# A four-layer gated cross-attention and feed-forward program on one core: another order of work in the first expert layer

## The reference

```
x = x + tanh(g_xattn[n]) * attention_n(layernorm(x), ctx)
x = x + tanh(g_ffn[n])   * ffn_n(layernorm(x))
```

```
scores = sigmoid(x @ gate_w.T)                 # 64 experts in 8 groups; 4 groups are kept
idx, w = top 6 of the kept experts, w scaled to sum 2.5
shared = relu(x @ su.T)**2 @ sd.T              # 512 hidden features, for every token
slot   = rank of the token among the tokens of its expert; 64 slots per expert
yd[e]  = relu(xd[e] @ w1[e].T)**2 @ w2[e].T    # xd[e]: the 64 token rows of expert e
out    = shared + sum over the 6 experts of w * yd[e, slot]
```

## Time and profile before

| | us |
|---|---|
| median of 3 runs | 2621.82 |
| range | 2613.22 to 2622.74 |
| profiled execution | 2621.67 |
| its span | 2619.9 |
| TensorE busy in the span | 2358.4 (90%) |

### The profile page before, as it was taken

One profiled execution on the slowest core, in us unless ns is written; L12 is line 12 of the kernel. 1 busy time (PEld: TensorE's weight loads), 2 busy tenths in 40 slices (PEclk: granted clock), 3 DMA queues, 4 the chain that ended last, 5 costly groups with the idle time before them and its releaser, 6 DMA issues. The chain is left out here.

```text
span 2619.9 us, 31016 instructions
## 1 busy us (share of the span) xinstructions
PE 2358.4 (90%) x11508; PEld 1603.2 (61%) x11508; DVE 1589.5 (61%) x2529; ACT 1044.5 (40%) x1517; POOL 1452.7 (55%) x850
## 2 busy tenths in 40 slices
PE   7879999899999986699799999969997999999778
PEld 6657777655555544466455555567886555555467
DVE  4654442367777756966677777632225777777442
ACT  3433333244545432411344545423332554554333
POOL 1431110057878874346387878843442687887733
PEclk9889898599999997689799999979998999999879
DMA  1034443301111103100111111022211111111010
GB/s 33 1 123 141 136 148 120 97 18 54 36 51 38 36 9 131 36 14 1 54 36 53 36 52 37 7 62 71 89 37 48 36 36 52 38 36 42 1 51 20
DMA packets 50128, 138.52 MB, mean 53 GB/s; under 512 B 7757, under 2 KB 13597, under 8 KB 49404
## 3 DMA queue, kind: packets, MB, share of 16 engines
q1 hardware_dynamic: 49596, 136.22, 16.9%
q10 hardware_dynamic: 384, 0.33, 0.1%
HBM read 123.32 MB, written 13.21 MB: 52 GB/s over the span
## 5 line engine op out<-in xcount | busy, mean ns | idle before, releaser
L2080 DVE TENSOR_REDUCE mx<-psum 128x1 f32<-128x500 f32 x1008 | 643.8, 675 | 248.0 <-PE psum L1186 245.6
L1615 ACT ACTIVATE E<-psum 125x896 f32<-125x896 f32 x576 | 527.5, 919 | 665.8 <-PE psum L1207 657.0
L1843 POOL TENSOR_TENSOR SA<-SA,E 125x896 f32<-125x896 f32 x288 | 611.3, 2123 | 22.6
L1215 PE MATMUL psum<-E,V 125*64 125x448 f32 x2304 | 472.4, 545 | 0.0
L1186 PE MATMUL psum<-K,Q 128*128 128x500 f32 x1008 | 370.1, 416 | 30.3 <-DVE mx L2080 9.4
L1205 PE MATMUL psum<-Q,K 128*125 128x448 f32 x1152 | 345.7, 381 | 8.9 <-DVE Q L2020 7.2
L1207 PE MATMUL psum<-Q,K 128*125 128x448 f32 x1152 | 329.6, 367 | 0.0
L1843 POOL TENSOR_TENSOR SA<-SA,SB 125x896 f32<-125x896 f32 x96 | 202.6, 2111 | 194.6 <-DVE SB L2100 190.5
L1215 PEld LDWEIGHTS psum<-E,V 125*64 125x64 f32 x2304 | 152.6, 136 | 231.0 <-issue 221.4
L1205 PEld LDWEIGHTS psum<-Q,K 128*125 128x125 f32 x1152 | 203.0, 187 | 136.4 <-issue 107.2
L1186 PEld LDWEIGHTS psum<-K,Q 128*128 128x128 f32 x1008 | 192.2, 191 | 139.0 <-DVE mx L2080 74.8
(11 more groups left out here) (295 smaller groups left out, 3848.5 us busy)
## 6 DMA issues: line engine op xcount, KB each, us to landing
K<-kt_scratch SPq DMA_DIRECT2D x48, 750.0 KB, 5.0
K<-kt_scratch SPq DMA_DIRECT2D x48, 375.0 KB, 6.1
EW<-in_f_w SPq DMA_DIRECT2D x64, 256.0 KB, 6.7
kt_scratch<-kt SPq DMA_DIRECT2D x16, 750.0 KB, 4.2
WS<-in_f_w SPq DMA_DIRECT2D x31, 384.0 KB, 5.4
WoT<-in_a_WoT SPq DMA_DIRECT2D x24, 256.0 KB, 2.6
V<-in_ctx SPq DMA_DIRECT2D x16, 375.0 KB
Wq<-in_a_Wq SPq DMA_DIRECT2D x16, 256.0 KB, 3.0
```

The costliest lines, as they stand in the source:

```text
L1215: i = e.matmul(psum[c * DC:(c + 1) * DC, 4 + b % 2, 0:HT], V[0:LP, b, k * DC:(k + 1) * DC], E[g[n, b, k] % NE][0:LP, half[c]], start=k == ...
L1615: e.activation(E[m % NE][0:LP, :].rearrange("p (c q) -> p c q", c=2), psum[0:LP, pair:pair + 2, 0:HT], ACT.Exp).then_inc(exp_set.sem, 1)
L1843: e.tensor_tensor(SA[b % 2][0:LP, :], a[0:LP, :], x[0:LP, :], ALU.add).then_inc(sum_set.sem, 1)
L2080: e.tensor_reduce(mx[:, b % 2, j * 3 + c:j * 3 + c + 1], psum[:, bank, 0:CW], AX.X, ALU.max).then_inc(small_free.sem, 1)
```

## The change

Five things are changed, all in this stage or just ahead of it:

1. Router weights, shared weights and a new small table `slots` are loaded during the projection stage before, and DVE splits the router weights there, after its fourth tile. The copies of the tokens become a task of their own (`tokens`) at k = 5 of the dense part.
2. The table `slot_rows` is no longer loaded and rounded. DVE makes the selectors of one group in one instruction of 128 x 512 (`rows`), 8 in all, in two buffers.
3. `st` is made in four parts of 2, 2, 2 and 1 tiles, where it was two parts of 4 and 3, and PE waits for each part by itself.
4. The context is rotated two batches ahead (`crot` and `cadd` of b+2 during batch b), `cadd` moves one step forward, and a side item stands after every step; the context work then ends with the first step of group 6.
5. Folding is staggered (`fg` one pair behind, `fa` two) with three buffer sets; 14 of its 32 steps stand in group 7, 4 before `back` 0, 6 before `back` 1 and 8 behind it.

```diff
 def context_order():
-    steps = [[("cload", 0), ("cload", 1)], [("crot", 0)], [("cadd", 0)]]
+    steps = [[("cload", 0), ("cload", 1)], [("crot", 0)], [("cadd", 0), ("cload", 2)], [("crot", 1)], [("cadd", 1)]]
     for b in range(B):
         first = [("cstore", b - 1)] if b > 0 else []
-        first += [("cload", b + 2)] if b + 2 < B else []
-        first += [("crot", b + 1)] if b + 1 < B else []
-        last = [("cadd", b + 1)] if b + 1 < B else []
-        steps += [first + [("cturn", b, 0)], [], [("cturn", b, 1)], [], last + [("cturn", b, 2)]]
+        first += [("cload", b + 3)] if b + 3 < B else []
+        first += [("crot", b + 2)] if b + 2 < B else []
+        last = [("cadd", b + 2)] if b + 2 < B else []
+        steps += [first + [("cturn", b, 0)], [], [("cturn", b, 1)], last, [("cturn", b, 2)]]
...
+def folding_ahead():
+    pairs, steps = H // 2, []
+    for p in range(pairs + 2):
+        steps += [[("fu", 1, p)], [("fm", 1, p)]] if p < pairs else []
+        steps += [[("fg", 1, p - 1)]] if 0 <= p - 1 < pairs else []
+        steps += [[("fa", 1, p - 2)] + ([("fload", 1, p + 1)] if p + 1 < pairs else [])] if p >= 2 else []
+    return steps
...
+        if k == 5:
+            order.append(("tokens",))
         if k == len(slots):
             order.append(("route", 5))
-    order += [("wload", e) for e in range(4, 12)]
-    order += [("route", 6), ("st", 0, 0), ("st", 0, 1), ("route", 7), ("route", 8), ("disp", 0, 0), ("disp", 0, 1),
-              ("st", 1, 0), ("st", 1, 1)]
+    order += [("wload", e) for e in range(4, 12)] + side.pop(0)
+    order += [("route", 6)] + [("st", 0, a) for a in range(4)] + [("route", 7), ("rows", 0), ("disp", 0, 0), ("route", 8), ("disp", 0, 1)]
+    order += [("st", 1, a) for a in range(4)]
...
-            if n not in (3, 7) and side:
+            if (g, n) == (NG - 2, 12):
+                order.append(("fload", 1, 0))
+            if side:
                 order += side.pop(0)
+                if not side:
+                    order += [("fload", 1, 1), ("fload", 1, 2)]
+            elif g == NG - 1:
+                order += last.pop(0)
     order.append(("comb", E0 // 2 - 1))
-    order += [t for step in side for t in step]
-    last = list(last)
-    order += [t for step in last[:8] for t in step] + [("back", 0)]
-    return order + [t for step in last[8:] for t in step] + [("back", 1)]
+    order += [t for step in last[:4] for t in step] + [("back", 0)]
+    order += [t for step in last[4:10] for t in step] + [("back", 1)]
+    return order + [t for step in last[10:] for t in step]
...
-FOLD_BUFS = {1: 2, 2: 1, 3: 1}
+FOLD_BUFS = {1: 3, 2: 1, 3: 1}
...
+        if n == 0:
+            e.dma_start(ffn[0]["GW"][:, :, :], io["f0_gate"]).then_inc(gate_in.sem(0), 16)
+            for k in range(NS0):
+                e.dma_start(ffn[0]["WS"][k][:, :], io["f0_w"][k]).then_inc(ws_in.sem(0, k), 16)
+            e.dma_start(ffn[0]["slots"][:, :], io["slots"]).then_inc(slots_in.sem(), 16)
...
+            elif kind == "rows":
+                g, = t
+                k0 = 2 * CAP0
+                if g >= 2:
+                    e.wait_ge(*matched.at(4 * (g - 2) + 3, 1))
+                e.scalar_tensor_tensor(m["rows"][g % 2][:, :, :], m["slots"][:, k0:k0 + 8].unsqueeze(2).broadcast_to([P, 8, CAP0]),
+                                       m["slots"][:, k0 + 8 + g:k0 + 9 + g], m["slots"][:, CAP0:k0].unsqueeze(1).broadcast_to([P, 8, CAP0]),
+                                       ALU.is_equal, ALU.mult).then_inc(rows_set.sem, 1)
```

More of the change, by code:

```diff
@@ L126, in constants @@
     c["blockdiag2"] = bd
[L127 to L131, removed]
+    slot = np.tile((np.arange(CAP0) - CAP0 // 2).astype(f), (P, 1))
+    parts = [slot, np.where(np.arange(P)[:, None] < E0, f(1.0), -2.0 * slot), np.tile(np.arange(8, dtype=f), (P, 1)),
+             (np.arange(P)[:, None] % E0 - 8 * np.arange(NG)[None, :]).astype(f), 1.0 - slot.T[np.arange(P) % CAP0, 0:1] ** 2]
+    c["slots"] = np.concatenate(parts, 1).astype(f)
     rows = np.arange(64)[:, None] % 32
@@ L198, in expert_order @@
     return order + [("back", 1)]
+def folding_ahead():
[5 more added lines that the diff above has]
+    return steps
 def sparse_order(side, last):
     order = [("fetch", n) for n in range(NS0)] + [("logits", 0), ("logits", 1), ("split", 0), ("split", 1)]
-    slots = [(n, c) for n in range(NS0) for c in range(2)]
+    slots, side, last = [(n, c) for n in range(NS0) for c in range(2)], list(side), list(last)
     for k in range(len(slots) + 3):
@@ L570, in build @@
         m[name] = [mem.take(name, [P, HT], d) for _ in range(4)]
+    w_at = mem.at
+    assert w_at >= parts_end
+    for name, d in (("WS", F32), ("WH", F32R), ("WL", F32R)):
+        m[name] = [mem.take(name, [P, 512], d) for _ in range(NS0)]
+    after_w = mem.at
+    m["GW"], m["GH"], m["GL"] = (mem.take("gate_" + n, [P, KD, E0], d) for n, d in (("w", F32), ("hi", F32R), ("lo", F32R)))
+    m["slots"] = mem.take("slots", [P, CAP0 * 2 + 17], F32)
+    at(w_at)
+    m["OT"] = mem.take("OT", [P, KD, T], F32)
+    at(w_at)
+    m["EW"] = [mem.take("EW", [P, 512], F32) for _ in range(3 * NS0)]
+    assert mem.at == after_w
     at(st_end)
@@ L576, in build @@
     kt = [mem.take("kt", [P, L], F32R) for _ in range(2)]
+    assert mem.at <= w_at
+    at(st_at)
+    fold_bufs[1] = fold_tiles(1, 1)
+    assert mem.at <= st_end
     at(side_at)
-    fold_bufs[1] = fold_tiles(1)
-    at(mh_at)
+    fold_bufs[1] += fold_tiles(1, 2)
+    assert mem.at <= w_at
+    at(folded_at)
     m["ST"].append(mem.take("ST", [P, NT, 512], F32R))
[L581 to L585, removed]
     assert mem.at <= base
+    at(norm_at - 2 * 4 * 512)
+    m["rows"] = [mem.take("slot_rows", [P, 8, CAP0], F32R) for _ in range(2)]
     at(yh_at)
@@ L759, in build @@
     fold_loads = [(n, p) for n in layers for p in range(H // 2)]
-    ring = lambda name, per, loads: Landed(nc, name, 2, [(p % FOLD_BUFS[n], (n, p)) for n, p in loads], per)
+    ring = lambda name, per, loads: Landed(nc, name, 3, [(p % FOLD_BUFS[n], (n, p)) for n, p in loads], per)
     fold_r, fold_m = ring("fold_r", 1, fold_loads), ring("fold_m", 2, fold_loads)
@@ L775, in build @@
     gate_in, sel_in = one("gate_w", 1, [(f,) for f in experts]), one("sel", 1, [(f,) for f in (2, 3)])
-    rows_in = one("slot_rows")
-    slots_in = one("slots", 2)
+    slots_in = one("slots")
     ew_in = Landed(nc, "ew", 12, [(e % 12, (e,)) for e in range(E0)])
@@ L1361, in pe_experts @@
                     e.wait_ge(*gt_set.at(f, 1))
-                    e.wait_ge(*rows_act.at())
-                    e.wait_ge(*rows_pool.at())
-                e.matmul(psum[:, bank, 0:HT], m["rows"][:, q * P:(q + 1) * P], m["GT"][:, half[c]], start=True, stop=True).then_inc(matched.sem, 1)
+                e.wait_ge(*rows_set.at(q // 4))
+                pair = m["rows"][q // 4 % 2][:, q % 4 * 2:q % 4 * 2 + 2, :].rearrange("p k c -> p (k c)")
+                e.matmul(psum[:, bank, 0:HT], pair, m["GT"][:, half[c]], start=True, stop=True).then_inc(matched.sem, 1)
             elif kind == "comb":
@@ L1699, in act_experts @@
                 e.activation(m["XD"][g % 2][:, kd, :], psum[:, upper_bank[f, (kind, g, kd)], :], ACT.Copy).then_inc(xd_set.sem, 1)
-            elif kind == "route" and f == 0 and t[0] == 5:
-                e.wait_ge(*rows_in.at())
-                e.activation(m["rows"][:, 0:2048], m["rows_raw"][:, 0:2048], ACT.Copy).then_inc(rows_act.sem, 1)
             elif kind == "ups":
@@ L1892, in pool_experts @@
                 e.tensor_tensor(rot[0:LP, :, d:DC], x[0:LP, :, 0:d], sin3[:, :, d:DC], ALU.mult).then_inc(rot_set.sem, 1)
[L1893 removed]
+            elif kind == "tokens":
                 e.wait_ge(*tokens_high.at())
                 e.tensor_tensor(m["YtL"][:, :, :], Y[:, :, :], m["YtH"][:, :, :].bitcast(F32), ALU.subtract).then_inc(tokens_low.sem, 1)
[L1896 to L1898 removed]
             elif kind == "back" and f != 3:
```

92 lines of the change are left out of this document (38 added, 54 removed).

## The result

The changed kernel took 2574.65 us (median of 4 runs, 2573.85 to 2581.62), the kernel before 2617.92 (4 runs, 2613.22 to 2622.74, beside it on the same chip). The ratio is 0.9841 with a 95% interval of 0.9812 to 0.9869: 43 us or 1.6% faster. 2585 was predicted, with a range of 2573 to 2604. The profiled execution took 2574.31 us, its span is 2572.5.

A forecast was written before the change was run, and what follows sets the result against it. TensorE, busy in 90% of the span, was taken as the bound. Head -7.5, router split +0.5, dense part 0, groups' idle time -14, clock -5, folding -10.5 sum to -36.5 against 2621.67: 2585 us, range 2573 to 2604.

The forecast's parts named there:

- the third rival: Folding tail: the clock stays up through it, 26.9 us taking 16.5, time 2575 us; chance 0.06.
- The head: Stage start: first `up` at 144.5 us instead of 151.99, through earlier router weights and shorter waits; -7.5 us.
- the dense part's 0: Dense part: `tokens` delays and savings on slots and masks cancel; 0 us, bounds -3 and +2.5.
- The +0.5 for the router split in the stage ahead: Projection stage: DVE's router split, moved there, costs +0.5 us, bounds 0 and 2.4.
- The groups' idle time: Sparse groups before the last: TensorE's idle time falls, less a one-time start cost; -14 us, bounds -18 and -6.
- The 12.4 us go: Sparse groups: rotating two batches ahead removes TensorE's 8 waits for DVE's last rotary sum, 12.4 us.
- most of the other 6.4: Sparse groups: half masks remove most of 6.4 us of waits for a PSUM bank behind a busy DVE.
- The clock: Sparse groups: less time at the lower clock without the two longest stalls; -5 us, bounds -10 and +3.
- Folding and the end: Group 7 and after: folding steps in group 7 run at full clock; -10.5 us, bounds -1 and -21.
- The first: Group 7: folding keeps the clock low or waits for banks; fold term about 0, 2596 us; chance 0.14.
- The second, waits that change owner: Sparse groups: TensorE waits for DVE's `kt` instead; idle term -3, clock term 0, 2601 us; chance 0.14.
- the fourth: Sparse groups: context transfers come too late, DVE held 2.9 us per batch, 41 us, 2626 us; chance 0.03.

The follow-up runs named there:

- late-loads kernel: Changed kernel with router, dense weights and slots loaded at the stage's start and the router split there; 2582.08 us, ratio 0.985.
- all three back: Changed kernel with rotation one batch ahead, old side-item places and masks in halves at their old places, as before; 2596.96 us, ratio 0.9913.
- halves: Changed kernel with masks in two halves at the places they had before; 2592.31 us, ratio 0.9902.
- pairs at the old places: Changed kernel, masks still in four parts but issued two together where a half stood before; 2592.86 us, ratio 0.9891.
- before, masks in four parts: Kernel before with only the masks changed, to four parts at the new places; 2595.26 us, ratio 0.9902.
- one batch ahead: Changed kernel with the context rotated one batch ahead again, side items at their new places; 2580.67 us, ratio 0.9842.
- rotation and places back: Changed kernel with rotation one batch ahead and no side items after steps 3 and 7, as before; 2570.39 us, ratio 0.9815.
- rotation back, tokens first: Changed kernel with rotation one batch ahead and the split of the tokens ahead of the logits; 2569.93 us, ratio 0.9807.
- tokens first: Changed kernel with the split of the normalised tokens put ahead of the logits; 2573.03 us, ratio 0.9825.
- halves at the new places: Changed kernel with masks in two halves, behind the `disp` steps and ahead of `downs`; 2578.04 us, ratio 0.9837.
- folding behind: Changed kernel with all folding behind the last `comb` in the old step order, three buffer sets; 2588.74 us, ratio 0.9872.
- old places: Changed kernel with no side item after steps 3 and 7 of a group, as before; 2574.72 us, ratio 0.9815.

## Why the prediction was right, and where it was not

**The number: partly luck.** 2574.65 us lies in the stated range, 1.7 us above its lower end, and outside the forecast's own 2577 to 2594. It is the time that the third rival gave, 2575, whose mechanism did not occur. The head and the folding were right; the sum of the groups held only because one cause was wrong and its size right, and the clock gave more than twice what was said.

**The head: right.** The first `up` came at 144.57. From it to the groups it took 36.1 us, before 36.7, so the dense part's 0 held too: -8.0 for both against -7.0, or -8.3 from each stage's own beginning. The row of 4.36 us was missed; it runs beside the HL wait that I had priced. The late-loads kernel gives the loads 2.7 us, where I had put 2.5. In that kernel the first `up` still comes 5.0 us earlier than before, counted from the stage's beginning (10.8 against 15.9). Its head differs from the old one chiefly in that GpSimd's 4 us split no longer stands ahead of `WL`; that this is the cause was argued from the earlier trace rows and not tried alone. The +0.5 for the router split in the stage ahead cannot be seen: that stage's end moves by 2.3 us between executions.

**The groups' idle time: right in size, wrong in cause.** "The 12.4 us go" was argued from the rotation two batches ahead, and the mask parts were given "most of the other 6.4". Idle time fell by 14.7 (-14 said). But with the rotation back only 5.2 us of V waits return, with 2.1 us of idle time, and with the masks alone on the old kernel 12.4 falls to 5.8 and idle time by 12.1. The step that failed is the one from the row of waits to its reason: the row names the last releaser, DVE's sum, and I took what feeds the sum (GpSimd's rotation) for what delays it. DVE's own rows just ahead of the sum were the ones to read. Two batches ahead, the sum is early enough to pass such a delay, which is why the V waits go by that way too; but the delay then falls on the next copy, and the gain is small. That the size came out is luck.

**The clock: the mis-sized term.** -5 was said, with -10 as its bound. It came to -13.1, the busy time that groups 0 to 6 lost without losing work. I had counted the two drops that began in the longest stalls and kept the other seven. I also called the 242 us of the earlier trace rows the groups before the last; they hold 13.7 us of group 7, and a group took 33.5 us, not 34.6, which changes no term by much. Busy and idle time of these groups in all kernels:

| kernel | idle us | busy us |
|---|---|---|
| before | 18.6 | 216.0 |
| all three back | 16.5 | 213.9 |
| halves | 11.1 | 213.3 |
| pairs at the old places | 11.0 | 211.6 |
| before, masks in four parts | 6.5 | 203.0 |
| one batch ahead | 6.2 | 207.2 |
| rotation and places back | 6.0 | 201.5 |
| rotation back, tokens first | 5.8 | 201.5 |
| tokens first | 5.0 | 204.7 |
| halves at the new places | 4.6 | 207.2 |
| folding behind | 4.1 | 203.1 |
| after | 3.9 | 202.9 |
| late loads | 3.4 | 210.9 |
| old places | 2.1 | 206.1 |

With some 11 us of idle time or more, busy time is 211.6 to 216.0, with under 7 it is 201.5 to 207.2, but for the one kernel with 210.9; under 7 no order is left in it. Between before and after each microsecond of idle time taken away gave 0.9 more by the clock. Why the late loads' groups ran at the lower clock for longer is open.

**Folding and the end: right in its parts.** -10.5 was said, -14.6 is the difference of the windows and 14.1 the time that the kernel with the folding behind took more. Group 7 grew by 11.1 (12.8 said) at a clock of 1.00, so the steps there ran at full speed and waited for no bank. Behind the last `comb` 40.0 us passed (42.2 said): `back` 0 held TensorE for 2.2 (2.6), `back` 1 for 11.05 (11.6), the last read-out for 0.98 (1.1), and the 18 steps took 25.7 (26.9), since the clock held for longer: 1.00 until 421, 5.6 us behind the last `comb`, where 4.9 had been seen before.

**The rivals.** The first is refuted by the 1.00 in group 7. The third, the clock up through the tail, is refuted by the row of 440.90 to 455.35: TensorE was busy for 13.47 of 14.45 us, and the clock was 0.50. The rule of the Trainium skill (TensorE: Matmul & The Clock Gate, "The two states you'll see") ties the lower clock to idleness and the higher to sustained work, and in these stretches it is not borne out. That the clock was low at 440.90 fits it, since TensorE had been busy for only 1.47 of the 4.90 us before; that it stayed low through the busy stretch does not. In the kernel before, the clock fell after a busy stretch and stayed down for a mostly busy one:

```profile
440.12:445.00 4.88, 4.42 (x39) 3.71 (x40) 0.79 (x2) 1.42 (x4) 0.00 (x0) 1.00 0.31 94
449.00:494.00 45.00, 41.29 (x182) 34.22 (x182) 9.66 (x27) 9.32 (x27) 1.76 (x3) 0.50 0.30 93
```

The second, waits that change owner, came in small: 3.4 us in four waits. It comes larger where masks stand at the old places beside the new rotation (`kt`, 4.9 us at one line, idle time 11.1). Of the fourth, 74.3 us of GpSimd's waits for transfers are there, but not its price: DVE waited for the rotation 11.3 us in 8 waits, hardly more than the 10.4 in 8 before, and no wait of TensorE is put down to either. That the two batches between rotation and turn absorb them was argued, not tried.

**Sum.** Against the prediction the head came 1.0 us lower, groups 0 to 6 8.8 lower (8.1 of it the clock), folding and the end 4.0 lower, and later stages 2.9 higher, where nothing had been expected: 10.9 by the profiled executions, 2585.2 to 2574.3. In those later stages TensorE was busy for the same time (1929.9 us before, 1929.3 after) and waited for longer, 2.6 us of it for DVE's `h` at one line (14.3 us before, 16.9 after); why is open.

## What to carry to other kernels

In an engine that works in order, place long work that nobody needs soon ahead of an instruction that will wait, not behind it: the same mask halves, one step earlier, were worth 14 us here. For a wait on a short instruction, read the releaser's own rows just before it, what ran and what it waited for, before naming a cause. And where the mean clock stands between its levels, as in these groups, allow for idle time of TensorE to cost up to about twice its length (here 14.7 us of it went with 13.1 us of busy time), but undo one part at a time before giving a gain to any of them.

## What the runs showed of the hardware

- A DVE operation with two inputs in SBUF took 4.36 us beside GpSimd's 4.04 us operation, and 0.62 us without it, in the kernel with tokens first. The rule of the Trainium skill (SBUF — State Buffer, "Who interferes with whom"), of which no row had shown this case, holds: DVE's operation, which started 0.17 us after GpSimd's, ended half a microsecond after GpSimd's end at 165.66. GpSimd lost nothing to speak of, 4.04 against 3.99 us in the kernel with tokens first.
- Folding steps of the same form took 0.89 and 0.65 us among `comb` matmuls of 448 columns, 1.54 and 1.12 in a stretch of their own, in which TensorE was busy for 93% of the time. The granted clock was 1.00 (2.4 GHz) in the first stretch and 0.50 (1.2 GHz) in the second.
- Two kernels with the same code in groups 0 to 6 and nearly the same idle time there (3.9 and 3.4 us) differed by 8 us of busy time in them (202.9 at a mean clock of 0.95, 210.9 at 0.91).
